# Token stages of a two-layer transformer: the values' tail product on four array tiles, and the second norm's rows on ScalarE

## The chip, the cores and the metric

The kernel runs on one core of a Trainium2 chip. Its time is the device time of one execution, in microseconds (us). The engines have short names here: PE (TensorE, matrix products; PEld is its weight load), DVE (VectorE), ACT (ScalarE), POOL (GpSimd) and SP (SyncE, which issues DMAs). Each runs its own list of instructions strictly in order and waits for the others by semaphores. A matrix product takes a stationary operand (up to 128 rows by 128 columns of the array) and streams a moving one through it, up to 512 columns at a time, into PSUM, which has eight banks of 512 f32 columns on 128 partitions.

## The reference, cut to what matters

Four sequences of 2048 tokens (8192 tokens of width 512) pass through two layers. Each adds a cross attention to a context of 154 keys, then a second part, which is a mixture of experts in the first layer and a light and heavy feed-forward with routing in the second.

```
x = x + attn0(layernorm(x), ctx)          # 16 heads of 32, 154 keys, softmax
x = x + experts(layernorm(x))             # top 8 of 32, gate = layernorm(x) @ gate.T
x = x + attn1(layernorm(x), ctx)
y = layernorm(x)
x = x + light(y) + heavy(y)               # score = y . routing_token
attn:  p = softmax((q k^T * tau + delta) / sqrt(32));  out = (p v) Wo^T + bo
```

Only the two attention stages with the norm behind them are touched here.

## The kernel before, in words

`token_phase` is run twice, once for each layer; `gate` is true in the first. A stage goes through NG = 16 groups of 512 tokens (TG = 4 tiles of 128). A turn i works at the same time on four groups: it prepares the queries of group i + 1 (norm, transposes by `x_turn`, product with wq), does the attention of group i, projects the output of group i - 1 and adds it to x (`residual`), and does the side work of j = i - 2, which is the second norm `z` and, in the first stage, the gate: `z_turn` transposes z on PE, and `gate_parts` multiplies it with the gate's weights.

A turn has 16 units, and each unit is one of the four tiles for one of the four head groups g (four heads each). A unit takes two steps of the counter `at`, which runs from 0 to 31. The order of every engine's work inside a turn is written out by hand in tuples of `at` values (V for the values products, Z for z's transposes, NZ for z's rows, OO and OL for the attention output, PT for the tails' copy, QO for the queries' copy). A smaller number stands earlier in the turn, and within one `at` the order of the `if` lines holds.

For one unit, `scores` (four products of 154 columns into a ring over banks 0 to 2) is followed by `maximum` on DVE, four exponentials with their sums on ACT, `inverse` on DVE and `normalize` on POOL. Then `p_transposes` on PE turns the probabilities of the first 128 keys into bank 4 (four transposes), and DVE or ACT copies them to pTm. The last 26 keys of each head are the tail: POOL packs them for four heads into 104 columns, a fifth transpose turns them into bank 5, and ACT copies them to pTt once per head group. `values` then computes p v for 512 tokens of one head group: one f32 product over the 104 tail rows into all 128 output rows, against a value table `vt` with zeros where the heads don't match, and four f32 products of 32 output rows each over the 128 main keys, which run side by side. Both go to bank 7. ACT copies the result (`o_out`), and DVE subtracts to get its low part (`o_low`). An f32 product is carried out as two passes, so the rows show x2 for the tail product and x8 for the four main ones.

Queries and projections use bank 6 (A_BANK), so each query product waits until ACT has copied the one before it (`query_out`). They are sums of three products of 512 columns (L81 to L83, the helper `product`) for each of four chunks; `streamed` issues two chunks in each odd step.

The second norm: DVE gathers the statistics, POOL computes `rstd` (L607, L609), and DVE writes z = (x - mean) * rstd (L722), four instructions per group, in steps 0, 0, 1, 1 of the first stage and 3, 7, 10, 13 of the second. `z_turn` for the first quarter stands at step 3 on PE and waits for all four rows.

## Time and profile before

| | us |
|---|---|
| median of 3 runs | 3379.52 |
| lowest and highest | 3376.65, 3384.28 |
| the profiled execution, its own time | 3375.24 |
| span of its core in the trace | 3373.5 |

Over the span PE was busy for 94%, DVE for 81%, POOL for 62% and ACT for 46%. The first token stage fills about 105 to 955 us, the experts follow until about 1850 us, the second token stage fills about 1955 to 2740 us, and the rest is the light and heavy part. A turn takes 52.6 us in the first token stage and 50.4 us in the second, and turns repeat almost to the hundredth of a microsecond. Busy time says little about PE here, since its products overlap: the distance between the starts of two products is the measure of what one costs.

### The profile page before, as it was taken

The page shows a single profiled execution, that of the slowest core. Times are in us where ns is not written, and L with a number is a line of the kernel's source. Part 1 is how long each engine was busy: PE and PEld are TensorE (multiplying, and loading weights), DVE is VectorE, ACT ScalarE, POOL GpSimd, SP SyncE. Part 2 cuts the span into 40 slices and gives each one's busy share as a digit, 9 for nine tenths or more (in the row PEclk, how much of TensorE's full clock was granted, in tenths as well). Part 3 has the DMA queues.
Part 4 walks back from the last instruction along what each step waited for, and adds up shares of the span by engine and source line. Part 5 has one row for each costly group of instructions (what it writes and reads, how often), then busy time and mean ns, then how long its engine had stood idle before and what let it go on. Part 6 is the DMA issues. An engine that isn't in the chain of part 4 may idle for free. (4 is left out here: it accounts for less than half of the span.)

```text
span 3373.5 us, 55546 instructions
## 1 busy us (share of the span) xinstructions
PE 3187.6 (94%) x17270; PEld 2498.1 (74%) x17270; DVE 2720.3 (81%) x5412; ACT 1560.8 (46%) x5463; POOL 2097.0 (62%) x2416
## 2 busy tenths in 40 slices
PE   7999999999979999999999699999999969999998
PEld 5677777777647888888888567777777758778886
DVE  4788888889746888888887389999999879967775
ACT  1766666676621111111111377777777745321111
POOL 1766766667635777777777477777777753433333
PEclk8999999999989999999999899999999989999999
DMA  7345454454465666766676444555554457730111
GB/s 219 100 137 169 119 172 134 141 155 134 136 210 131 167 176 165 179 168 166 166 179 155 111 128 135 159 164 144 150 171 136 138 166 287 274 102 13 26 13 25
DMA packets 285026, 491.01 MB, mean 146 GB/s; under 512 B 54258, under 2 KB 75058, under 8 KB 284018
## 3 DMA queue, kind: packets, MB, share of 16 engines
q1 hardware_dynamic: 252146, 409.92, 39.3%
q0 software_dynamic: 32256, 77.65, 12.3%
q8 instruction: 116, 1.90, 0.2%
q14 instruction: 124, 1.02, 0.1%
q10 hardware_dynamic: 384, 0.52, 0.1%
HBM read 250.32 MB, written 136.96 MB: 115 GB/s over the span
## 5 line engine op out<-in xcount | busy, mean ns | idle before, releaser
L984 ACT ACTIVATE c_pr<-ps,t_negmax 128x154 f32<-128x154 f32 x1024 | 384.8, 392 | 197.3 <-DVE t_negmax L731 196.3
L731 DVE TENSOR_REDUCE t_negmax<-ps 128x4 f32<-128x616 f32 x512 | 404.1, 789 | 53.2 <-PE ps L1053 52.7
L984 ACT ACTIVATE t_pr<-ps,t_negmax 128x154 f32<-128x154 f32 x1024 | 384.8, 392 | 107.9 <-DVE t_negmax L731 103.0
L754 DVE COPY t_pTm<-ps 128x512 f32<-128x512 f32 x448 | 306.2, 683 | 118.6 <-PE ps L1066 114.5
L649 POOL TENSOR_TENSOR t_pr<-t_pr,t_inv 128x512 f32<-128x512 f32 x256 | 274.8, 1073 | 191.0 <-DVE t_inv L746 189.9
L649 POOL TENSOR_TENSOR c_pr<-c_pr,t_inv 128x512 f32<-128x512 f32 x256 | 271.7, 1061 | 195.2 <-DVE t_inv L746 193.9
L1053 PE MATMUL ps<-t_kst,t_stack 98*128 98x154 f32 x2048 | 352.8, 291 | 26.7 <-DMA t_stack<-t_q_low 10.0
L1053 PEld LDWEIGHTS ps<-t_kst,t_stack 98*128 98x128 f32 x2048 | 279.5, 193 | 39.1 <-issue 18.3
L81 PE MATMUL ps<-e_xT_high,e_wgu_high 128*128 128x512 f32 x768 | 301.6, 393 | 1.4 <-DVE e_xT_low L1639 1.4
L83 PE MATMUL ps<-e_xT_high,e_wgu_low 128*128 128x512 f32 x768 | 299.3, 390 | 0.0
L82 PE MATMUL ps<-e_xT_low,e_wgu_high 128*128 128x512 f32 x768 | 299.0, 389 | 0.0
L1686 ACT ACTIVATE e_sig<-ps 128x512 f32<-128x512 f32 x96 | 57.3, 597 | 499.4 <-PE ps L83 494.6
L81 PE MATMUL ps<-t_xnT_high,t_wq_high 128*128 128x512 f32 x512 | 221.8, 433 | 18.2 <-ACT t_qT L907 18.2
L2341 POOL TENSOR_TENSOR h_w_low<-c_hw,h_w_high 128x512 fp32r<-128x512 f32 x64 | 89.8, 1403 | 232.8 <-DVE h_w_high L70 232.8
L81 PE MATMUL ps<-t_wo_high,t_oT_high 128*128 128x512 f32 x512 | 218.2, 426 | 0.4 <-DVE c_wide_rows L763 0.4
L984 ACT ACTIVATION_READ_ACCUMULATOR t_pr<-ps,t_negmax 128x1 f32 x1024 | 213.2, 208 | 0.0
L984 ACT ACTIVATION_READ_ACCUMULATOR c_pr<-ps,t_negmax 128x1 f32 x1024 | 212.5, 208 | 0.0
L1296 POOL TENSOR_TENSOR e_wd_low<-c_wd_in,e_wd_high 128x512 fp32r<-128x512 f32 x96 | 131.1, 1391 | 127.2 <-DVE e_wd_high L70 127.2
L621 POOL TENSOR_TENSOR t_q_low<-t_qT,t_q_high 128x512 fp32r<-128x512 f32 x128 | 170.5, 1332 | 54.7 <-DVE t_q_high L70 54.7
L83 PE MATMUL ps<-t_xnT_high,t_wq_low 128*128 128x512 f32 x512 | 203.5, 397 | 0.0
L82 PE MATMUL ps<-t_xnT_low,t_wq_high 128*128 128x512 f32 x512 | 202.6, 396 | 0.0
L83 PE MATMUL ps<-t_wo_high,t_oT_low 128*128 128x512 f32 x512 | 201.4, 393 | 0.0
(359 smaller groups left out, 9313.8 us busy)
## 6 DMA issues: line engine op xcount, KB each, us to landing
t_stack<-t_q_high SPq DMA_DIRECT2D x1016, 64.0 KB, 2.0
c_wgu_in<-in_gate_upT SPq DMA_DIRECT2D x32, 1536.0 KB, 6.4
t_stack<-t_q_low SPq DMA_DIRECT2D x512, 64.0 KB, 2.0
x_dram<-c_wide_rows SPq DMA_DIRECT2D x32, 1024.0 KB, 7.6
c_wd_in<-in_downT SPq DMA_DIRECT2D x32, 768.0 KB, 11.5
t_xbo<-in_x SPq DMA_DIRECT2D x16, 1024.0 KB, 5.7
xw_dram<-t_z SPq DMA_DIRECT2D x16, 1024.0 KB, 5.3
t_xbo<-x_dram SPq DMA_DIRECT2D x16, 1024.0 KB, 11.2
```

The costliest lines, as they stand in the source:

```text
L81: pe.matmul(out, left[0], right[0], start=start, stop=False)
L82: pe.matmul(out, left[0], right[1], start=False, stop=False)
L83: return pe.matmul(out, left[1], right[0], start=False, stop=stop)
L621: pool.tensor_tensor(qlow[:, n % 2, :], qT[:, n % 2, :], qhigh[:, n % 2, :].bitcast(F32), ALU.subtract).then_inc(s["q_low"], 1)
L649: pool.tensor_tensor(main, main, inv[:, v, :].unsqueeze(2).to_broadcast([P, HG, P]), ALU.mult).then_inc(s["normed"], 1)
L731: dve.tensor_reduce(negmax[:, u, :], flat[:, at:at + HG * APART].rearrange("p (h n) -> p h n", h=HG)[:, :, 0:KEYS], AX, ALU.max, negate=Tr ...
L754: dve.tensor_copy(pTm[:, g % 2, :, t * P:(t + 1) * P], ps[:, 4, :].rearrange("p (h n) -> p h n", h=HG)).then_inc(s["pTm"], 1)
L984: op = act.activation(pr[:, u % 4, h, :], flat[:, col:col + KEYS], ACT.Exp, bias=negmax[:, u, h:h + 1], accum_out=total[:, u, h:h + 1])
L1053: mm = pe.matmul(flat[:, at:at + KEYS], stack[:, HG * (g % 2) + h, t * P:(t + 1) * P], kst[:, g, h * KEYS:(h + 1) * KEYS], start=True, sto ...
L1296: pool.tensor_tensor(wd[1][:, f, :], c["wd_in"][:, f, :], wd[0][:, f, :].bitcast(F32), ALU.subtract).then_inc(s["wd_low"], 1)
L1686: act.activation(sig[:, (FC * q + f) % 2, :], ps[:, b, :], ACT.Silu).then_inc(s["silu"], 1)
L2341: pool.tensor_tensor(w1[1][:, m % RING], c["hw1"][:, :, f * P:(f + 1) * P], w1[0][:, m % RING].bitcast(F32), ALU.subtract).then_inc(s["w1" ...
```

## The change

It has two parts.

The first is on the values. The tails of a pair of heads now form a block of 52 rows (PROWS), and the blocks of the two pairs stand at partitions 0 and 64, so a tile's tails take 116 columns. Their transposes leave `p_transposes` and become `tail_transposes`, four in a row once per head group, at the new steps TT. The tail product becomes four products of 64 rows by 64 columns of the array over 256 tokens each: two pairs of heads times two halves of the 512 tokens. So that the four fall on four different tiles, `place` swaps the pairs for the last two token tiles. The output goes to banks 5 and 6, 256 columns each, the main products are split in two halves as well (eight instead of four), and A_BANK moves to bank 7. Bank 5 thus holds the tails' transposes and then half of the output, so the transposes of a group wait for `o_low` of the one before.

The second is on the norm. The rows of z are now made by ACT (`side_rows`, an Identity with scale rstd and bias shift = -mean * rstd), at steps 0, 1, 2, 3 of the first stage and 1, 4, 8, 10 of the second. POOL computes shift with two more small instructions. `z_turn` moves from steps 3, 5, 8 to 4, 6, 9. `residual` and `rstd_of` get a wait for the rows of z. The inverse of the sums is written in place.

```diff
+        def place(h, t):
+
+            return h if t < TG // 2 else (h + 2) % HG
...
-        V = (15, 24, 2, 7) if gate else (15, 23, 3, 6)
+        V = (15, 24, 2, 7) if gate else (15, 23, 1, 7)
+        TT = (12, 20, 30, 5) if gate else (12, 20, 29, 5)
...
-        Z = (3, 5, 8, 22)
+        Z = (4, 6, 9, 22)
...
-        OL = (23, 30, 4, 9) if gate else (17, 27, 5, 9)
+        OL = (18, 27, 4, 9) if gate else (17, 26, 3, 9)
...
-        NZ = (0, 0, 1, 1) if gate else (3, 7, 10, 13)
+        NZ = (0, 1, 2, 3) if gate else (1, 4, 8, 10)
...
-        OO = (16, 26, 2, 7) if gate else (15, 24, 4, 7)
+        OO = (16, 25, 2, 7) if gate else (15, 24, 2, 7)
...
+                    reached(pool, s["z" if gate else "xl"], TG * n)
...
+                    pool.tensor_scalar(shift[:], mv[:, which, :, 0], -1.0, None, ALU.mult).then_inc(s["s_minus"], 1)
+                    pool.wait_ge(s["s_minus"], n + 1)
+                    pool.wait_ge(s["s_rstd"], n + 1)
+                    pool.tensor_tensor(shift[:], shift[:], rstd[:, which, :], ALU.mult).then_inc(s["s_shift"], 1)
...
+                if v % TG == 0:
+                    reached(pool, s["tail_mm"], GROUPS * i + v // TG - 1)
...
+                    reached(dve, s["z" if gate else "xl"], TG * j)
...
+            def side_rows(j, t):
+                act.wait_ge(s["s_shift"], j + 1)
+                if t == 0 and (gate or j < NG - 1):
+                    reached(act, s["z_stored"], 16 * j)
+                if t == 0 and gate:
+                    reached(act, s["z_mm"], DC * j)
+                act.activation(z_of(j)[:, t, 0:D], xs[:, t, :], ACT.Identity, bias=shift[:, t:t + 1],
+                               scale=rstd[:, 1, t:t + 1]).then_inc(s["z" if gate else "xl"], 1)
...
-                if t == 0:
-                    reached(pe, s["pTt"], GROUPS * i + g)
                 for h in range(HG):
-                    pe.transpose(ps[:, 4, h * P:(h + 1) * P], pr[:, v % 4, h, 0:P], ident[:])
-                pe.transpose(ps[0:TROWS, 5, t * P:(t + 1) * P], tails[:, v % 4, :],
-                             ident[:]).then_inc(s["p_mm"], 1)
+                    mm = pe.transpose(ps[:, 4, h * P:(h + 1) * P], pr[:, v % 4, place(h, t), 0:P], ident[:])
+                mm.then_inc(s["p_mm"], 1)
+
+            def tail_transposes(i, g):
+
+                pe.wait_ge(s["normed"], 2 * (UNITS * i + TG * g + TG))
+                reached(pe, s["oT_out"], GROUPS * i + g)
+                for t in range(TG):
+                    at = (HIGH + PROWS) * ((TG * g + t) % 8)
+                    mm = pe.transpose(ps[0:HIGH + PROWS, 5, t * P:(t + 1) * P], tails[:, at:at + HIGH + PROWS], ident[:])
+                mm.then_inc(s["tail_mm"], 1)
...
-                pe.matmul(ps[:, B_BANK, :], vt[:, g * P:(g + 1) * P], pTt[:], start=True, stop=False,
-                          skip_group_check=True)
-                for h in range(HG):
-                    mm = pe.matmul(ps[h * DK:(h + 1) * DK, B_BANK, :], vm[:, g * P + h * DK:g * P + (h + 1) * DK],
-                                   pTm[:, g % 2, h, :], start=False, stop=True, skip_group_check=True)
+                for half in range(2):
+                    for q in range(2):
+                        r = HIGH * (q if half == 0 else 1 - q)
+                        pe.matmul(ps[HIGH * q:HIGH * (q + 1), 5 + half, 0:HALF],
+                                  vt[r:r + PROWS, g * P + HIGH * q:g * P + HIGH * (q + 1)],
+                                  pTt[r:r + PROWS, half * HALF:(half + 1) * HALF], start=True, stop=False,
+                                  skip_group_check=True)
+                for half in range(2):
+                    for h in range(HG):
+                        mm = pe.matmul(ps[h * DK:(h + 1) * DK, 5 + half, 0:HALF],
+                                       vm[:, g * P + h * DK:g * P + (h + 1) * DK],
+                                       pTm[:, g % 2, h, half * HALF:(half + 1) * HALF], start=False, stop=True,
+                                       skip_group_check=True)
...
```

What stands in a row on PE in steps 2 to 5 of a turn of the first stage, before (the L81 to L83 rows are the streamed query products, `t_z` the transposes of z, `c_pr` those of the probabilities):

```order
L1076 MATMUL ps<-t_pTt,t_vt 128x512
L1079 MATMUL ps<-t_pTm,t_vm 32x512 x4
...
L83 MATMUL ps<-t_xnT_high,t_wq_low 128x512
L1038 MATMUL ps<-ident,t_z 128x128 x4
L1065 MATMUL ps<-ident,c_pr 128x128 x4
L1066 MATMUL ps<-ident,t_tails 104x128
L1053 MATMUL ps<-t_kst,t_stack 128x154 x4
L81 MATMUL ps<-t_xnT_high,t_wq_high 128x512
```

and the same place of the change:

```order
L1113 MATMUL ps<-t_pTt,t_vt 64x256 x4
L1119 MATMUL ps<-t_pTm,t_vm 32x256 x8
...
L84 MATMUL ps<-t_xnT_high,t_wq_low 128x512
L1091 MATMUL ps<-ident,c_pr 128x128 x4
L1081 MATMUL ps<-t_kst,t_stack 128x154 x4
L1066 MATMUL ps<-ident,t_z 128x128 x4
L82 MATMUL ps<-t_xnT_high,t_wq_high 128x512
```

The transposes of z moved behind the transposes of the probabilities and the scores of unit 2, the tails' transpose left the row, and the values are two groups of smaller products.

ACT in steps 0 to 4 of the same turn, before (`t_qT` is the queries' copy, `t_oT_high` that of the attention output, each pair of `c_pr` rows the four exponentials of a unit):

```order
L907 ACTIVATE t_qT<-ps,t_bq 128x512 [waits t0_q_low,t0_q_mm]
L984 ACTIVATE c_pr,t_total<-ps,t_negmax 128x154 [waits t0_p_mm,t0_negmax]
L984 ACTIVATE c_pr,t_total<-ps,t_negmax 128x154 x3
L914 CAST t_oT_high<-ps 128x512 [waits t0_proj,t0_pv]
L907 ACTIVATE t_qT<-ps,t_bq 128x512 [waits t0_q_low,t0_q_mm]
L984 ACTIVATE c_pr,t_total<-ps,t_negmax 128x154 [waits t0_p_mm,t0_negmax]
L984 ACTIVATE c_pr,t_total<-ps,t_negmax 128x154 x3
```

and in the change:

```order
L923 ACTIVATE t_qT<-ps,t_bq 128x512 [waits t0_q_low,t0_q_mm]
L971 ACTIVATE t_z<-c_wide_rows,t_shift,t_rstd 128x512 [waits t0_z_mm,t0_z_stored,t0_s_shift]
L1010 ACTIVATE c_pr,t_total<-ps,t_negmax 128x154 [waits t0_p_mm,t0_negmax]
L1010 ACTIVATE c_pr,t_total<-ps,t_negmax 128x154 x3
L971 ACTIVATE t_z<-c_wide_rows,t_shift,t_rstd 128x512 [waits t0_s_shift]
L930 CAST t_oT_high<-ps 128x512 [waits t0_proj,t0_pv]
L923 ACTIVATE t_qT<-ps,t_bq 128x512 [waits t0_q_low,t0_q_mm]
L971 ACTIVATE t_z<-c_wide_rows,t_shift,t_rstd 128x512 [waits t0_s_shift]
L1010 ACTIVATE c_pr,t_total<-ps,t_negmax 128x154 [waits t0_p_mm,t0_negmax]
L1010 ACTIVATE c_pr,t_total<-ps,t_negmax 128x154 x3
L971 ACTIVATE t_z<-c_wide_rows,t_shift,t_rstd 128x512 [waits t0_s_shift]
```

Four rows of z now stand between the copies and the exponentials, the third and the fourth of them behind the second copy of the queries.

PE at the start of a turn of the second stage, before:

```order
L1065 MATMUL ps<-ident,t_pr 128x128 x4
L1066 MATMUL ps<-ident,t_tails 104x128
L1053 MATMUL ps<-t_kst,t_stack 128x154 x4
...
L83 MATMUL ps<-t_xnT_high,t_wq_low 128x512
L1076 MATMUL ps<-t_pTt,t_vt 128x512
L1079 MATMUL ps<-t_pTm,t_vm 32x512 x4
L1065 MATMUL ps<-ident,t_pr 128x128 x4
```

and in the change:

```order
L84 MATMUL ps<-t_xnT_high,t_wq_low 128x512
L1113 MATMUL ps<-t_pTt,t_vt 64x256 x4
L1119 MATMUL ps<-t_pTm,t_vm 32x256 x8
L1091 MATMUL ps<-ident,t_pr 128x128 x4
L1081 MATMUL ps<-t_kst,t_stack 128x154 x4
```

The values of head group 2 moved from behind unit 1's scores and query products (step 3) to in front of those scores (step 1).

## Rows read from the trace of the kernel before

**Rows 1.** Stretches of the token stages: busy us by engine, clock, DMA share, GB/s

```profile
105.00:955.00 850.00, 818.49 (x5024) 610.99 (x5022) 714.46 (x1636) 563.32 (x2320) 577.26 (x759) 0.99 0.49 143
1955.00:2740.00 785.00, 754.42 (x4535) 566.56 (x4528) 725.56 (x1483) 604.29 (x2404) 582.21 (x686) 1.00 0.50 145
```

**Rows 2.** Waits of PE in 105 to 955 us: us in total, times, longest

```profile
PE ps L1065 <- DVE t_pTm L754: 11.0, 15, 1.8
```

**Rows 3.** The same view in 1955 to 2740 us

```profile
PE ps L81 <- ACT t_qT L907: 12.2, 15, 0.9
```

**Rows 4.** Timeline of PE, one values step: start us, us, engine, line, operation

```profile
412.88 0.40 PE L83 MATMUL ps<-t_wo_high,t_oT_low 128*128 128x512 f32 x1
413.12 1.02 PE L1076 MATMUL ps<-t_pTt,t_vt 104*128 104x512 f32 x2
414.07 1.06 PE L1079 MATMUL ps<-t_pTm,t_vm 128*32 128x512 f32 x8
415.07 0.66 PE L1065 MATMUL ps<-ident,c_pr 128*128 128x128 f32 x4
```

**Rows 5.** Timeline of PE around the first side transposes of a turn, first token stage

```profile
446.74 0.39 PE L83 MATMUL ps<-t_xnT_high,t_wq_low 128*128 128x512 f32 x1
446.97 0.60 PE L1038 MATMUL ps<-ident,t_z 128*128 128x128 f32 x4
447.40 0.60 PE L1065 MATMUL ps<-ident,c_pr 128*128 128x128 f32 x4
447.84 0.27 PE L1066 MATMUL ps<-ident,t_tails 128*104 128x128 f32 x1
447.87 0.75 PE L1053 MATMUL ps<-t_kst,t_stack 98*128 98x154 f32 x4
448.45 0.43 PE L81 MATMUL ps<-t_xnT_high,t_wq_high 128*128 128x512 f32 x1
```

**Rows 6.** Timeline of ACT in the same stretch

```profile
447.17 0.69 ACT L907 ACTIVATE t_qT<-ps,t_bq 128x512 f32<-128x512 f32 x1 [0.97 <-PE ps L83]
447.75 0.38 ACT L984 ACTIVATE c_pr<-ps,t_negmax 128x154 f32<-128x154 f32 x1
...
449.21 0.60 ACT L919 COPY t_pTt<-ps 104x512 f32<-104x512 f32 x1
```

**Rows 7.** Groups by line, 105 to 955 us: busy us, mean ns, idle before

```profile
L722 DVE TENSOR_SCALAR t_z<-c_wide_rows,t_mv,t_rstd 128x512 f32<-128x512 f32 x64 | 45.0, 746 | 0.0
```

**Rows 8.** The same view in 1955 to 2740 us

```profile
L722 DVE TENSOR_SCALAR t_z<-c_wide_rows,t_mv,t_rstd 128x512 f32<-128x512 f32 x60 | 63.1, 1051 | 0.0
...
L961 ACT ACTIVATE t_z<-t_z,t_rn 128x512 f32<-128x512 f32 x56 | 39.6, 735 | 15.6 <-POOL t_rn L686 15.6
```

**Rows 9.** Timeline of POOL at the end of a turn, first token stage

```profile
436.50 0.20 POOL L607 TENSOR_TENSOR t_ve<-t_mv,t_eps 128x4 f32<-128x4 f32 x1 [2.03 <-DVE t_mv L717]
436.78 1.02 POOL L609 TENSOR_TENSOR t_rstd<-t_ve,t_half 128x4 f32<-128x4 f32 x1
437.77 1.04 POOL L649 TENSOR_TENSOR c_pr<-c_pr,t_inv 128x512 f32<-128x512 f32 x1
438.77 0.38 POOL L651 TENSOR_TENSOR t_tails<-c_pr,t_inv 128x104 f32<-128x104 f32 x1
```

**Rows 10.** Timeline of PE there

```profile
439.47 0.60 PE L1065 MATMUL ps<-ident,c_pr 128*128 128x128 f32 x4
```

**Rows 11.** Timeline of PE at the start of a turn, second token stage

```profile
2472.00 0.65 PE L1053 MATMUL ps<-t_kst,t_stack 98*128 98x154 f32 x4
...
2473.92 1.02 PE L1076 MATMUL ps<-t_pTt,t_vt 104*128 104x512 f32 x2
...
2476.88 0.43 PE L81 MATMUL ps<-t_xnT_high,t_wq_high 128*128 128x512 f32 x1
```

**Rows 12.** Timeline of ACT there

```profile
2473.71 0.39 ACT L984 ACTIVATE t_pr<-ps,t_negmax 128x154 f32<-128x154 f32 x1 [1.37 <-DVE t_negmax L731]
...
2475.18 0.70 ACT L907 ACTIVATE t_qT<-ps,t_bq 128x512 f32<-128x512 f32 x1
```

More of the change, by code:

```diff
@@ L414, in last, with halves @@
             return isinstance(j, int) and j == NG - 1
+        def place(h, t):
+            return h if t < TG // 2 else (h + 2) % HG
+        def halves(v):
+            return v.rearrange("p (b n) -> p b n", b=2)
         def o_bank(j, t):
@@ L596, in _ @@
             pool.memset(eps[:], EPS).then_inc(s["ready"], 1)
+            pool.memset(tails[:], 0.0).then_inc(s["ready"], 1)
             if gate:
@@ L601, in _ @@
                 pool.memset(c["z_last"][:, :, D:XS], 0.0).then_inc(s["ready"], 1)
[L602 removed]
+            pool.wait_ge(s["ready"], 3 if gate else 5)
             def rstd_of(which, kind, n):
                 pool.wait_ge(s[kind + "_mv"], TG * n + TG)
+                if kind == "s":
+                    reached(pool, s["z" if gate else "xl"], TG * n)
                 pool.tensor_tensor(ve[:, which, :], mv[:, which, :, 1], eps[:], ALU.add).then_inc(s[kind + "_ve"], 1)
@@ L1012, in turn @@
                         x_turned(i + 1, XT.index(at))
+                    if at in NZ and prev2:
+                        side_rows(j, NZ.index(at))
                     if at in ZA and gate and prev2:
@@ L1189, in turn @@
                         streamed(st)
+                    if at in TT[:3] and cur:
+                        tail_transposes(i, TT.index(at))
+                    if at == TT[3] and prev:
+                        tail_transposes(i - 1, GROUPS - 1)
                     if at in V[:2] and cur:
```

86 lines of the change are left out of this document (42 added, 44 removed).

## The prediction

> **What bounds the kernel now.** I read the busy times of the two token stages first, since nothing else of the kernel is edited except small work at its start. PE is busy for 818 of 850 us in the first stage and 754 of 785 us in the second, at full clock; DVE follows with 714 and 726, and ACT has 563 and 604 [rows 1]. PE's waits are short and repeat once a turn: 11.0 us in 15 waits for DVE's copy of the probabilities in the first stage [rows 2], and 12.2 us in 15 waits for ACT's copy of the queries in the second [rows 3]. So a stage is PE's list of products end to end plus some 2 us of waits in a turn of 50. A product saved on PE is time saved, but only as long as PE doesn't wait for something else afterwards. The question is therefore what each part takes from PE's list, and which wait the new places of ACT's work put into it.
>
> **The values.** Before, one values step takes 415.07 - 413.12 = 1.95 us from the first tail product to whatever follows [rows 4]. Four transposes of 128 columns take 447.84 - 447.40 = 0.44 us [rows 5], so 128 f32 columns cost 0.11 us and a pass of 512 costs 0.44. Two passes for the tails and two for the main keys (four products side by side) make 1.76 us, and the remaining 0.19 goes with the two changes of the array's division, about 0.10 each. Afterwards there are two passes of 256 columns for the tails, if the four tiles run side by side, and four of 256 for the main keys: 6 x 0.22 = 1.32 us. The divisions change three times, 0.29 us. That gives 1.61 us and a saving of 0.34. More pass boundaries, and weight loads that have only 0.22 us to hide under, take something back. No row shows their price; I bound it by 0 and by two more changes (0.20), and take 0.07, nearer to nothing, since the eight products of a values step already start together in rows of 1.06 us [rows 4]. The saving is 0.27 us a step (0.14 to 0.34), 1.08 a turn with four steps, 17 us a stage with 64. The tails' transposes are still four in a head group at 0.11 us each; they move and cost nothing more. Their new wait for the low part of the former output is hidden: ACT's and DVE's steps for it are over two units (some 6 us) before, except at step 5, where I still find 3 us between.
>
> A page bears on how the tiles share banks. The first two tail products come from row halves 0 and 64 of the array and both write bank 5, on partitions 0 to 63 and 64 to 127. The Trainium skill, TensorEngine Tiling (Array Packing), Restrictions and Gotchas, says that different row tiles cannot access the same PSUM bank simultaneously. No row here has row tiles, so the trace can't say; by that rule the tails cost what the first rival says.
>
> **The second norm's rows, first stage.** DVE loses 64 instructions of 746 ns, 45 us in all [rows 7]. DVE doesn't bound there, and its chain in front of the one regular wait [rows 2] (norm of x, copies, the second query cast) starts from PE's own transposes and isn't shortened. ACT gains as many, and I price them by its scaling of such rows from and to SBUF in the other stage: 735 ns, the next starting about 0.62 us after it [rows 8]. What matters is where they stand. Before, the query product of step 3 ends and the transposes of z follow at once, at 446.97 [rows 5], all z rows being done. ACT copies the queries at 447.17, begins the four exponentials of unit 1 at 447.75 and has them behind it at 449.21, 1.46 us later [rows 6]. Afterwards the third z row stands between the copy and the exponentials, the fourth behind them, and PE's transposes of z wait for the fourth. With the values 0.27 us shorter: copy at 446.90, third row at 447.48, exponentials at 448.10, fourth row at 449.56, done at 450.30. PE comes from the query product at 446.70, has 0.44 us of transposes and some 0.49 of scores, and would begin z's transposes at 447.62. It waits until 450.30, 2.7 us (on the way, the last of the scores waits for the first exponential, which is part of this). Before, this place lost 0.1 us [rows 5] (the scores took 0.58). So +2.6 us a turn. Nothing wins it back: the chain runs from PE through ACT to PE, and what DVE does later in the turn starts from PE's next transposes.
>
> POOL's two new instructions take about 0.28 us each, as its small one does (436.50 to 436.78), and stand in front of a unit's normalization that ends at 439.15 [rows 9], for which PE comes at 439.47 [rows 10]. About 0.5 later, less 0.3 of slack: +0.2 us a turn (0 to 0.5).
>
> A turn of the first stage: 2.6 + 0.2 - 1.08 = +1.7 us. 14 turns carry z rows beside attention: +24. Two turns have attention but no z rows: -2. First stage: **+22 us** (with a saving of 0.34 and no POOL term, +15; with 0.14 and 0.5, +33).
>
> **The second stage.** Here nobody waits for z early, and the rows stand apart. DVE, 92% busy, loses 63 us [rows 8], which shortens few of PE's waits, since those listed are for ACT [rows 3]. But the values of head group 2 move in front of unit 1's scores. Those started at 2472.00 [rows 11] and start 1.68 - 0.11 = 1.57 later. The exponentials of unit 1 go from 2473.71 [rows 12] to 2475.28, and the queries' copy behind them, 2475.18 before, to 2476.74, done at 2477.35. PE's next query product, at 2476.88 before [rows 11], is ready by 2476.39 (less 0.27, and two tail transposes of 0.11 that moved), so it waits 0.9 us. The values of group 3 move behind the query product of step 7, and their output copy stands before the queries' copy on ACT: 0.6 + 0.7 us after the values end, against 0.44 + 0.49 us of PE's work, a wait of 0.4. Together 1.3 - 1.08 = +0.2 us a turn: **+3 us** over 15 turns. If the relief of DVE takes 1 us a turn off the waits that remain, it is -13; if z rows and squares hold exponentials up once more in a turn, +12.
>
> **Start and ends.** In the last turns the four rows lie on ACT among its squares, where DVE made them beside it: 4 x 0.62 = 2.5 us, of which some is hidden: +2 us. POOL's clearing of the tails and two fewer DMAs for the value table lie beside the loading of inputs: 0 (-1 to +1).
>
> **The sum.** 22 + 3 + 2 = +27 us on the profiled execution's 3375.24: 3402. The median of the runs is 4.3 us above that execution, and the highest 9; I add half of the 4.3: **3404 us**.
>
> **Rivals.** (1) The four tiles don't run side by side, because pairs in one bank take turns: two more passes of 0.22 in each of 128 steps, +56 us, 3460. Against it: the four column tiles of the main product do share one bank now [rows 4]. Chance 0.08; it carries the page's rule. (2) Nearly even: the wait for z is there, but DVE's relief, 108 us over both stages [rows 7, 8], takes some 1 us a turn off the other waits, and the values save the full 0.34. 3404 - 16 - 9, about 3379. For it: DVE is the releaser in [rows 2]. Against: the DVE work in front of those waits isn't what is taken away. Chance 0.18. (3) Faster: ACT's rows bind nowhere, and only the saving is left, 128 x 0.27 = 35 us, 3340. It decides at the fourth row of z: if that is done before PE has finished the scores of unit 2, that is within 0.93 us of the query product's end, there is no wait; by the rows of ACT it takes 3.6. PE would have to carry 2.7 us less wait later in the turn, and the waits it has are about that long. Chance 0.12. (4) The second stage waits more for ACT, at 77% busy before and some 5 points more after: 3425. Chance 0.04. The forecast keeps 0.58.
>
> **How the numbers follow.** Leaving out (1) at the top and (3) at the bottom leaves 0.8: 3368, the low end of (2), to 3430, above (4) and the forecast's own upper bounds (22 to 33 and 3 to 12 make +20 on 3404). About 0.2%, 6.8 us, is what a measurement can tell from no change: 3372.8 to 3386.3. Faster takes (3) and 0.06 of (2); within takes the rest of (2) and 0.03 of the forecast: 0.15; slower takes the remainder, 0.67.
>
> **What would show it.** In the trace after, PE's transposes of z should wait about 1.7 us in each turn of the first stage for ACT's z rows, and the scores before them about 1 us for the exponentials; a first-stage turn should take 54.3 us instead of 52.6. The values step should take 1.68 us, with four tail products starting within hundredths of each other; if they start in two pairs 0.4 us apart, rival 1 holds. In the second stage the query product behind unit 2 should wait 0.9 us for its copy and the turn stay near 50.4 us. The forecast is wrong if the transposes of z don't wait, or if a turn of the first stage gets shorter.

## The result

The changed kernel takes 3429.99 us (median of 4, 3422.78 to 3435.32), the kernel before in the same comparison 3381.90 (median of 4, 3376.65 to 3390.04). The ratio is 1.0139, with a 95% interval of 1.011 to 1.0167: slower by some 48 us. The direction was forecast, but only +24.5 us of it (3404 against the median of 3379.52 that stood before); 3429.99 lies at the upper end of the range, 3368 to 3430. The profiled execution after is the fastest of its kernel (span 3421.0 us against 3373.5, +47.5).

The split by stage comes from the first and the last score matmul of each: the first token stage 838.6 to 870.9 us (+32.3), the second 798.7 to 811.7 (+13.0), between and around them +2.2. The forecast had +22, +3 and +2. All turn times below are measured from the first score matmul of unit 0 to that of the next turn. By that measure a turn of the first stage took 53.3 us before, not the 52.6 that the prediction gives; its "54.3 instead of 52.6" should be read as "+1.7". Nor do the turns of before all repeat to the hundredth: inner turns take 53.3 to 54.3 us in the first stage and 50.4 to 51.6 in the second.

The stretches of the changed kernel that answer to [rows 1], then two of its turns and one of before's (length, then busy us of PE, PEld, DVE, ACT, POOL, granted clock, DMA share, GB/s):

```profile
105.00:985.00 880.00, 809.55 (x5902) 626.59 (x5901) 676.09 (x1570) 606.67 (x2385) 572.26 (x789) 0.98 0.47 138
1985.00:2790.00 805.00, 744.99 (x5439) 575.72 (x5437) 692.91 (x1443) 647.50 (x2477) 575.27 (x721) 1.00 0.49 142
```

```profile
617.80:672.50 54.70, 51.18 (x384) 39.81 (x382) 44.13 (x104) 39.19 (x155) 36.96 (x52) 1.00 0.46 137
782.70:839.80 57.10, 53.04 (x383) 41.22 (x382) 44.35 (x104) 39.21 (x155) 36.98 (x52) 0.97 0.45 135
```

```profile
707.60:760.90 53.30, 52.23 (x327) 39.35 (x325) 46.37 (x108) 36.47 (x151) 37.14 (x50) 1.00 0.57 161
```

The work moved as the change says: DVE has 2 us less in a turn and ACT 3 more, and PE has 1 us less. The turn got longer all the same. PE's waits in the first stage (to be read against [rows 2]) and in the second (against [rows 3]):

```profile
PE ps L1066 <- ACT t_z L971: 26.3, 16, 4.4
PE ps L1081 <- ACT c_pr L1010: 19.4, 31, 1.1
PE ps L1091 <- DVE t_pTm L778: 10.2, 15, 0.7
```

```profile
PE ps L82 <- ACT t_qT L923: 34.5, 44, 1.0
PE ps L1081 <- ACT t_pr L1010: 15.1, 32, 1.2
```

The first two lines are the forecast wait for z's rows. Both are new: before, the first stage has no regular wait of the z transposes and 0.3 us in one wait for the exponentials. In the second stage the wait for the queries' copy has gone from 12.2 us in 15 waits to 34.5 in 44. A values step on PE, where [rows 4] shows one of before:

```profile
675.49 0.66 PE L1113 MATMUL ps<-t_pTt,t_vt 52*64 52x256 f32 x8
676.08 1.07 PE L1119 MATMUL ps<-t_pTm,t_vm 128*32 128x256 f32 x16
677.08 0.50 PE L82 MATMUL ps<-t_xnT_high,t_wq_high 128*128 128x512 f32 x1
```

It takes 677.08 - 675.49 = 1.59 us instead of 1.95. The four tail products take 0.59 us together, and their first passes begin within 0.02 us (675.489 to 675.509); had those of one bank taken turns, four passes of 0.22 would have made 0.88. So rival 1 is out: two row halves wrote one bank here, on different partitions, side by side. By the rule that it carried (the Trainium skill, TensorEngine Tiling (Array Packing), Restrictions and Gotchas) they would have taken turns; for this product the measurement decides against it.

The place in the first stage on which the forecast rests, PE and then ACT, in a turn of 54.7 us:

```profile
678.94 0.54 PE L1081 MATMUL ps<-t_kst,t_stack 98*128 98x154 f32 x3
680.59 0.34 PE L1081 MATMUL ps<-t_kst,t_stack 98*128 98x154 f32 x1 [1.11 <-ACT c_pr L1010]
682.40 0.55 PE L1066 MATMUL ps<-ident,t_z 128*128 128x128 f32 x3 [1.47 <-ACT t_z L971]
```

```profile
678.78 0.69 ACT L923 ACTIVATE t_qT<-ps,t_bq 128x512 f32<-128x512 f32 x1 [0.98 <-PE ps L84]
679.37 0.80 ACT L971 ACTIVATE t_z<-c_wide_rows,t_shift,t_rstd 128x512 f32<-128x512 f32 x1
680.07 0.38 ACT L1010 ACTIVATE c_pr<-ps,t_negmax 128x154 f32<-128x154 f32 x1
...
681.53 0.82 ACT L971 ACTIVATE t_z<-c_wide_rows,t_shift,t_rstd 128x512 f32<-128x512 f32 x1
```

```profile
L971 ACT ACTIVATE t_z<-c_wide_rows,t_shift,t_rstd 128x512 f32<-128x512 f32 x64 | 52.1, 822 | 2.1 <-POOL t_shift L630 2.1
```

The last line is the group of all such rows in the first stage, 105 to 985 us (busy us, mean ns). This is the chain as forecast: queries' copy, third row, exponentials, fourth row, z's transposes.

A turn of 57.1 us has the same two waits, of the same length. What differs is what follows them:

```profile
793.05 0.48 PE L82 MATMUL ps<-t_xnT_high,t_wq_high 128*128 128x512 f32 x1
793.36 0.41 PE L83 MATMUL ps<-t_xnT_low,t_wq_high 128*128 128x512 f32 x1
793.60 0.60 PE L84 MATMUL ps<-t_xnT_high,t_wq_low 128*128 128x512 f32 x1
794.00 0.63 PE L82 MATMUL ps<-t_xnT_high,t_wq_high 128*128 128x512 f32 x1
794.42 0.63 PE L83 MATMUL ps<-t_xnT_low,t_wq_high 128*128 128x512 f32 x1
794.85 0.63 PE L84 MATMUL ps<-t_xnT_high,t_wq_low 128*128 128x512 f32 x1
```

Passes of 512 columns start 0.23 us apart at first and then 0.43: the granted clock has fallen to its lower level, 1.2 GHz, and the turn's mean is 0.97. Four of the 13 turns between 174 and 895 us are so, and PE is busy 1.2 to 1.7 us longer in them. The last turn of the stage stands at 0.94. In the kernel before, no turn of the stage behind the first is below 1.00.

Against the same turns of the kernel before, the nine with full clock are longer by 1.6 us on average (0.5 to 2.3), the four with the fall by 2.7 to 3.75 and the last one by 4.6; the first two together by 0.5. So of the +32.3 us some 22 are what the turns cost at full clock, as forecast, and some 10 go with the fallen clock.

### The profile page after: what moved, and what is told of

Same layout as the page of the kernel before. It is cut to its first block and busy times, and to the rows that moved or that the text cites. A ratio compares the mean times of both kernels' runs of the same rounds, so it can differ in the third digit from the quotient of the medians.

```text
span 3421.0 us, 59457 instructions
## 1 busy us (share of the span) xinstructions
PE 3163.5 (92%) x19062; PEld 2520.8 (74%) x19062; DVE 2642.1 (77%) x5284; ACT 1645.4 (48%) x5591; POOL 2083.4 (61%) x2482
## 3 DMA queue, kind: packets, MB, share of 16 engines
q0 software_dynamic: 32256, 77.65, 12.2%
## 5 line engine op out<-in xcount | busy, mean ns | idle before, releaser
L668 POOL TENSOR_TENSOR t_pr<-t_pr,t_total 128x512 f32<-128x512 f32 x256 | 274.9, 1074 | 212.8 <-DVE t_total L770 211.4
L668 POOL TENSOR_TENSOR c_pr<-c_pr,t_total 128x512 f32<-128x512 f32 x256 | 271.0, 1058 | 215.3 <-DVE t_total L770 215.1
L83 PE MATMUL ps<-e_xT_low,e_wgu_high 128*128 128x512 f32 x768 | 299.3, 390 | 0.0
L83 PE MATMUL ps<-t_xnT_low,t_wq_high 128*128 128x512 f32 x512 | 204.4, 399 | 0.0
L83 PE MATMUL ps<-t_wo_low,t_oT_high 128*128 128x512 f32 x512 | 201.1, 393 | 0.0
```

The source lines that it names most:

```text
L83: pe.matmul(out, left[0], right[1], start=False, stop=False)
L668: pool.tensor_tensor(main, main, total[:, v, :].unsqueeze(2).to_broadcast([P, HG, P]), ALU.mult).then_inc(s["normed"], 1)
```

## The experiments

The theory after this comparison: in the first stage the rows on ACT cost a wait of 3 us a turn and now and then a fall of the clock; in the second stage the new place of the values costs. The rival: one part alone carries the loss in both. The table gives, for each kernel, the median time and from its trace the two stages and their usual turn (us). Each ratio is against the kernel before in the same comparison; its medians there lay from 3378.7 to 3381.9. The turn is one that recurs in the stage, with full clock (58.0 is the exception: that kernel has none with full clock; the 53.8 is one with fallen clock). It is mostly the shortest kind. The average over the fourth to the fifteenth of the first stage's 16 turns is 53.5 us before, 55.6 changed, 53.35 for the values only, 53.6 for z later and 53.0 for the values with xbo first (xbo is what the residual adds: the load of x's rows comes earlier there).

| kernel | time | ratio, 95% | first stage, turn | second stage, turn |
|---|---|---|---|---|
| before | 3381.9 | 1 | 838.6, 53.3 | 798.7, 50.4 |
| changed | 3430.0 | 1.011 to 1.0167 | 870.9, 54.7 | 811.7, 51.5 |
| values only | 3401.2 | 1.0046 to 1.0074 | 838.8, 52.6 | 823.2, 52.3 |
| rows only | 3451.5 | 1.0198 to 1.0225 | 908.0, 58.0 | 794.3, 50.1 |
| fill in the waits | 3425.4 | 1.0113 to 1.0144 | 867.6, 54.7 to 56.0 | 813.4, 51.6 |
| z later | 3397.4 | 1.0033 to 1.006 | 842.3, 52.6 | 813.9, 51.6 |
| group 2 back | 3433.3 | 1.0151 to 1.0186 | 878.0, 55.2 | 810.5, 50.4 to 53.8 |
| rows only, with fill | 3429.5 | 1.0132 to 1.0161 | 882.4, 56.5 | 795.5, 50.1 |
| values only, xbo first | 3395.2 | 1.0031 to 1.0057 | 832.6, 52.9 | 824.0, 52.3 |
| place only | 3404.5 | 1.0062 to 1.0086 | 840.5, 53.3 | 821.2, 52.0 |
| put together | 3371.0 | 0.9961 to 0.9982 | 836.3, 53.1 | 793.4, 49.9 |
| rows in second stage only | 3375.9 | 0.9983 to 1.0001 | 839.0, 53.3 | 794.7, 50.1 |
| put together, scaling later | 3367.8 | 0.995 to 0.9977 | 832.6, 52.9 | 786.6, 49.4 |
| before, no tail product | 3348.9 | 0.989 to 0.992 | 822.9, 51.7 | 790.0, 49.7 |

### The two halves apart

The changed kernel with the rows given back to DVE and `Z`, `ZD`, `ZA`, `NZ` and `SQ` as before (`ZD` and `ZA` are the steps at which DVE and ACT copy z's transposes out of PSUM, `SQ` those of ACT's squares):

```
-                    if at in NZ and prev2:
-                        side_rows(j, NZ.index(at))
...
+                        for t in range(TG):
+                            if at == NZ[t]:
+                                normed(1, "s", j, xs, z_of(j), "z" if gate else "xl", (t,))
```

> The changed kernel with the second half of the change taken back: the normalized rows are made by VectorE again, in the places of before; the split tail product and the tails' transposes once per group stay. Theory (the rows on ScalarE are what costs, the values part is a gain): the first stage has no wait of about 1.5 us before z's transposes and its turns are near 53.3 - 4 x 0.35 = 51.9 us; the second stage gains at most 1.4 us a turn, less if VectorE (busy 372.2 of 398 us before) becomes late; 3340 to 3365 us in all, faster than both kernels. Rival (the values part brings nothing because other engines are as late as PE): turns of 53.3 and 50.4 us as before, 3375 to 3385 us. Second rival (the values part costs as well, by its larger evictions and POOL's strided tails): above 3390 us.

And the kernel before with the rows alone:

> The kernel before with only the second half of the change: the normalized rows on ScalarE in the places of the changed kernel, POOL's two steps for the negated mean, z's transposes and evictions at the changed kernel's steps; tails and values as before. Theory (the two halves add up: the rows cost about 3 us of waits a turn in the first stage, now and then a fall of the granted clock behind them, and 1 to 2.5 us a turn in the second): first-stage turns of 56 us, 3445 to 3475 us in all. Rival (most of the rows' cost exists only because the values part has put other evictions of ScalarE into the same steps): first-stage turns near 54.5, 3395 to 3425 us.

Measured: 3401.2 and 3451.5. The first is a miss; the time lies in the second rival's range, but the place of the values, tested below, and not larger evictions or POOL's strides, gives most of it. The second falls in its range, though not by the parts expected: 58.0 us a turn in the first stage instead of 56, and a gain in the second instead of a loss. The values part, meant to save PE's time, is slower by itself, and wholly in the second stage: 823.2 us against 798.7, 52.3 us a turn against 50.4, with the same waits for the queries' copy as the changed kernel:

```profile
PE ps L82 <- ACT t_qT L924: 31.8, 41, 1.0
PE ps L1080 <- ACT t_pr L1011: 12.6, 26, 0.8
```

The rows cost nothing there: alone they make the second stage shorter by 4.4 us. In the first stage it is the other way about: the values part makes the usual turn 0.7 us shorter where it saves PE 1.4 (the average turn only 0.2, in part for a reason found below), and the rows alone cost 4.7 us a turn. They do so by waits of 2.0 and 1.0 us in all 13 inner turns (160 to 900 us), and in every one of these turns the granted clock falls:

```profile
PE ps L1047 <- ACT t_z L953: 25.5, 13, 2.0
PE ps L1062 <- ACT c_pr L991: 13.1, 13, 1.0
```

```profile
699.30:757.40 58.10, 54.33 (x328) 40.55 (x326) 44.26 (x104) 39.27 (x156) 37.23 (x52) 0.97 0.45 135
```

So the loss of the first stage is the rows', that of the second the values'. The halves don't add: 19.5 and 69.8 us alone, 48.1 together. With the values part the z wait is shorter (1.5 us against 2.0) and most turns keep their clock.

### Does standing still cost the clock?

The same edit in the changed kernel (8 and 12 transposes) and in the kernel with the rows alone (6 and 14). Bank 3 is where z's transposes go next:

```
+            def filler(j, n):
+                pe.wait_ge(s["logit"], j + 1)
+                pe.wait_ge(s["xnT_low"], DC * (j + 3))
+                for m in range(n):
+                    pe.transpose(ps[:, T_BANK, (m % TG) * P:(m % TG + 1) * P], ident[:], ident[:])
...
                 if k == 0:
+                    filler(j, 12)
                     pe.wait_ge(s["z"], TG * (j + 1))
```

> The changed kernel with work for TensorE put into the two waits of the first stage's turns: 8 transposes of the identity ahead of the last score matmul of unit 2 and 12 ahead of z's transposes, into the bank that z's transposes then overwrite. Both groups are shorter (0.9 and 1.3 us) than the waits there (1.3 and 1.7 us beyond the usual distance), so they should cost nothing by themselves. Theory (the fall of the granted clock to one half in four of the turns, 227.9, 338.6, 506.6 and 782.7, comes from TensorE's standing still just before): no turn with a granted clock under 0.99, four turns shorter by 1.7 us and the last one too, 7 to 10 us less than the changed kernel, so 3420 to 3424. Rival (the clock falls by something that has nothing to do with the waits): the same turns at 0.97 and 3428 to 3432 us. If the filler delays the real work, above 3435.

> The kernel before with the rows on ScalarE, as in the run of the rows alone (3451), and with 6 and 14 transposes of the identity in the two waits of 1.2 and 2.2 us in each turn of the first stage. There the granted clock is 0.97 or less in each of the turns that has these waits, and its passes of 512 columns take 427 ns for some 3 us behind them. Theory (standing still makes the clock fall, and this fall is a third of what the rows cost in the first stage): granted clock 1.00 in these turns, 56.3 instead of 58.0 us a turn, 13 turns, 3425 to 3432. Rival (the slow passes have another cause, such as the load of DMA or ScalarE at this place): clock 0.97 as before, 3448 to 3455.

Measured in the kernel with the rows alone: 3429.5 us, 22 less than without the fill, and the turn goes from 58.0 to 56.5 us, at full clock in every turn after the first:

```profile
682.30:738.90 56.60, 55.05 (x348) 41.28 (x345) 44.27 (x104) 39.27 (x156) 37.25 (x52) 1.00 0.44 127
```

In the changed kernel no turn after the first is below 1.00 either, and the last one takes 48.5 us instead of 52.6. The time is 4.6 us less, short of the 7 to 10 expected; its first turn took 51.7 us against 48.3, and without it the stage is 6.7 us shorter. That the fall follows PE's standing still is shown by the kernel with the rows alone (22 us). (The Trainium skill, TensorE: Matmul & The Clock Gate, The HAM clock gate, describes these two levels and that an idle array gets the lower one; the traces agree on the levels, with 0.43 and 0.23 us a pass, and here waits of 1 to 2 us are all the idleness that stands before a fall.) What decides between two turns with equal waits isn't: it fell in 4 inner turns of the changed kernel's trace and in 7 of the kernel with group 2 moved back, whose first stage has the same code. It fell behind a single wait too: one of 1.5 us for DVE's copy (at 400.6 us in the kernel without the tail product), one of 1.65 (at 2327.6 in the version put together) and one of 2.3 (at 2175.4 in the kernel with group 2 moved back). The other three executions of the changed kernel had a mean clock of 0.974 to 0.975 against 0.979 in the profiled one and took 7 to 13 us longer. So its median probably holds more falls than its trace.

### The wait for the fourth row

```
-        Z = (4, 6, 9, 22)
+        Z = (6, 8, 10, 22)
-        ZD = (5, 11)
+        ZD = (7, 11)
-        ZA = (7, 24)
+        ZA = (9, 24)
```

> The changed kernel with z's first three transposes of the first stage two steps, two steps and one step later (6, 8 and 10 in place of 4, 6 and 9) and their evictions with them (VectorE 7, ScalarE 9), so that the fourth row, which ScalarE finishes 0.2 us before they start now, has two steps more. Theory (the wait for the fourth row is half of what the rows cost, and is only a matter of its place): the 1.5 us before z's transposes go and nothing is late in their stead, the wait of 1.1 us for the exponentials stays, the granted clock falls less; first-stage turns near 53.2, 3398 to 3410 us. Rival (ScalarE is behind by its own work in steps 1 to 5, and PE only meets it somewhere else): PE waits for p copies, query copies or exponentials instead, 3420 to 3430 us.

Measured: 3397.4 us, 33 less, just under the range. PE's waits from 160 to 850 us:

```profile
PE ps L1081 <- ACT c_pr L1010: 14.5, 13, 1.1
PE ps L1066 <- ACT t_zT L954: 6.3, 13, 0.5
PE ps L1091 <- POOL t_tails L674: 5.9, 4, 1.9
```

The wait for z's rows is gone, and that for the exponentials stays. A smaller one stands in its stead, for ACT's copy of z's first transposes (0.5 us a turn). The wait for DVE's copy of the probabilities, 12.3 us in 12 with the values part alone over the same time, is gone too. The usual inner turn takes 52.6 us, as with the values part alone. So the loss was a matter of place: with the rows on ACT and z two steps later, the first stage (842.3) is within 3.5 us of the one with the rows on DVE (838.8).

### What costs in the second stage

Two runs take the place of the values step and its product apart. The place alone, in the kernel before:

```
-        V = (15, 24, 2, 7) if gate else (15, 23, 3, 6)
+        V = (15, 24, 2, 7) if gate else (15, 23, 1, 7)
-        OO = (16, 26, 2, 7) if gate else (15, 24, 4, 7)
+        OO = (16, 26, 2, 7) if gate else (15, 24, 2, 7)
-        OL = (23, 30, 4, 9) if gate else (17, 27, 5, 9)
+        OL = (23, 30, 4, 9) if gate else (17, 26, 3, 9)
```

> The kernel before with its own values product and rows, and only the places of the second stage moved as the change has them: values of group 2 at step 1 instead of 3 and of group 3 at 7 instead of 6, output copies at 2 and 7, low parts at 3 and 9. It is the other half of the run that puts group 2 back. Theory (the place costs by itself): TensorE waits 1.2 us behind unit 2's scores and 0.4 before the projection, a turn of the second stage takes 51.6 to 52.2 us instead of 50.4, 3398 to 3408. Rival (the place is harmless and the split product costs): 50.4 us a turn and 3380 to 3384.

And the split product with group 2 at its old place:

```
-        V = (15, 24, 2, 7) if gate else (15, 23, 1, 7)
+        V = (15, 24, 2, 7) if gate else (15, 23, 3, 8)
-        TT = (12, 20, 30, 5) if gate else (12, 20, 29, 5)
+        TT = (12, 20, 30, 5) if gate else (12, 20, 29, 6)
-        OO = (16, 25, 2, 7) if gate else (15, 24, 2, 7)
+        OO = (16, 25, 2, 7) if gate else (15, 24, 4, 8)
```

> The changed kernel with the values of head group 2 of the second stage back at step 3, where before had them (ScalarE's output copy at 4, VectorE's at 5), and group 3 behind them: its tails at step 6, its values at 8, copies at 8 and 10. Nothing else is moved. In the changed kernel TensorE stands still 1.2 us in each turn behind unit 2's scores, since the values no longer lie between the third query product and the fourth. Theory (in the second stage the place of this step costs, not the split product): that wait goes, a turn takes about 50.3 us instead of 51.5, 15 turns bring 15 to 20 us, 3408 to 3415. Rival (the turn is set by VectorE and ScalarE with the split product wherever it stands): 51.3 to 51.6 us a turn, 3425 to 3432.

The place alone costs 1.6 us a turn, 22.4 us in the stage, as expected, with the waits of the changed kernel (27.8 us in 43 for the queries' copy). It is the larger part of the answer. The waits make 1.1 of the 1.6 us in an inner turn; PE's own list is 0.5 us longer as well (49.5 against 49.0 us busy), which no run follows up. Before, the values of group 2 lay between the third query product and the fourth and covered the copy of the third. At step 1 they cover nothing, and the copy begins 8.5 us into the turn instead of 6.6 besides. In the changed kernel:

```profile
2468.59 0.66 PE L1081 MATMUL ps<-t_kst,t_stack 98*128 98x154 f32 x4
2470.25 0.50 PE L82 MATMUL ps<-t_xnT_high,t_wq_high 128*128 128x512 f32 x1 [1.01 <-ACT t_qT L923]
...
2477.50 0.50 PE L82 MATMUL ps<-t_wo_high,t_oT_high 128*128 128x512 f32 x1 [0.29 <-ACT t_qT L923]
...
2505.22 0.34 PE L1081 MATMUL ps<-t_kst,t_stack 98*128 98x154 f32 x1 [0.76 <-ACT t_pr L1010]
```

These are the two forecast waits (0.9 and 0.4 us) and one that wasn't. In all, the waits of this turn come to 3.5 us, those of a turn before to 1.3 (0.82 for the queries' copy and 0.46 for the exponentials). Of the 2.2 more, 1.3 were forecast. The other 0.9 are longer or new waits for the exponentials, the first copy of the queries and DVE's copy. Those for the exponentials come with the split product, not with the rows: 12.6 us in 26 waits with the values part alone, 6.1 in 13 with the place alone. So this is where the time that it saves on PE goes.

Putting group 2 back took the wait of 1.01 us away (14.6 us in 15 remain, which before has too) and gave nothing, a miss: 51.4 us a turn on average over the inner turns with full clock, and 1.2 us in the whole stage. (The time of the whole kernel is longer by what its first stage lost to the clock.) In its place stands a wait for which the profile names no releaser, ahead of the scores of unit 4:

```profile
PE ps L1081 <- issue: 16.9, 16, 2.4
PE ps L82 <- ACT t_qT L923: 14.6, 15, 1.0
```

```profile
2588.22 0.65 PE L1081 MATMUL ps<-t_kst,t_stack 98*128 98x154 f32 x4 [2.44 <-issue]
```

Unit 4 is the first of its group and needs the stack of group 1, the queries' parts as DMAs lay them out for the scores. The queue issues the last transfers of the low part until 2584.5 us, and these land a median of 3.6 us later, at 2588.1:

```profile
L485 SPq DMA_DIRECT2D t_stack<-t_q_low x4: 588/590/591, 2582.6 to 2584.5; - x4
...
DMA to landing us min/median/max: 3.4/3.6/4.5
```

So this is, by the times, the stack's transfer; the same sum fits a short wait in another turn (2482.1 + 2.0 to 2.6, the scores at 2484.18). Unit 4's scores start 14.6 us into the turn before, when the values of group 3 stand ahead of them; with those behind, PE is there after 12.5 us and waits until 12.9 to 15.2.

### How much of PE's saving arrives

> The kernel before without the tail keys' product in both stages (the tails are still normalized, transposed and copied, but not multiplied with the values; the attention over them is left out of the result). It takes from TensorE a pass of 0.44 us and one change of the array's division (0.10) in each of 128 values steps, 2.2 us a turn, and from no other engine anything. Theory (TensorE is the busiest engine but the turn is held by the loop through maximum, exponentials, normalization and copy, so what is saved on TensorE comes back as waits): the second stage's turn goes from 50.4 to no less than 49.8, the first's from 53.3 to about 52.3, 3353 to 3365. Rival (TensorE's list is the turn): 48.2 and 51.1 us a turn, 3312 to 3325.

Measured: 3348.9 us, a little under the theory's range and far above the rival's. Some 0.54 x 128 = 69 us were taken from PE and 31 arrive by the medians, 25 by the two traces. The usual turn is 1.6 us shorter in the first stage and 0.7 in the second, of 2.2. The stages as a whole gain 15.7 and 8.8 us of some 35 each, which is less, 1.0 and 0.5 a turn: the first turns of a new batch gain 0.5 to 0.8 us in the first stage, and in two inner turns of the first stage and one of the second the granted clock fell to 0.97. The rest stands in waits (1968 to 2680 us; before, the same lines have 1.7 and 6.1 us), and in others for DVE that come up (8.5 us in 22):

```profile
PE ps L1053 <- issue: 11.0, 13, 3.0
PE ps L1053 <- ACT t_pr L984: 8.4, 13, 0.6
```

### A load that POOL waits for

```
+                if cur:
+                    load_xbo(i)
                 if nxt and cur and (i + 1) % PER == 0:
                     load_values(sp, i + 1, 0)
...
-                if cur:
-                    load_xbo(i)
```

> The kernel with the values part alone (3401) and one order of the first stage's DMA queue changed: the load of the residual's rows goes ahead of the loads of the next batch's values and keys. With the values part POOL waits for this load in the first turn of each new batch (10.0 us in 3 times, 4.4 before), and TensorE's p transposes wait for POOL; those turns take 54.2 to 55.3 us instead of 52.6. Theory (the value table's third load in each group, and the earlier pace, put this load behind): the three turns take 52.6 to 53 us, 4 to 6 us less, near 3396. Rival (the queue waits for something ahead of these loads anyway): no difference, 3399 to 3403, or slower where the keys or values now come late.

Measured: 3395.2 us, 6 less; the two intervals overlap, but in the traces the first stage, the only one touched, is 6.2 us shorter. POOL's wait for the load falls from 10.0 us in 3 times to 0.2 in one, and the turns of 54.2 to 55.3 us are gone. That this load came late is shown. Why it did with the values part (two DMAs for the value table in a group where there was one, or the shorter turn) isn't taken apart.

### A version from these runs

> A version put together from what the runs show. First stage: the split product, the rows on VectorE as before, the residual's load ahead of the next batch's values (as in the run with that order, whose first stage took 832.7 us against 838.6 before). Second stage: the split product, the rows on ScalarE, and the values of group 2 at step 3 again, those of group 3 at step 7 (with their tails at 6), their output copy at 8, behind the queries' copy. With group 3 at step 8 the scores of unit 4 started so early that they waited for the stack's transfers (16.9 us in 16 waits); at 7 its product lies in front of them again. Theory (both covers are back: the product of group 2 hides one query copy, that of group 3 hides the stack's transfer): no wait behind unit 2's scores, no waits of 1 to 2.7 us ahead of unit 4's, turns of 49.6 to 50.4 us, 3352 to 3370 in all. Rival (the stack's transfer sets the turn as long as TensorE is quick in steps 1 to 7): waits ahead of unit 4's scores stay at 0.5 us or more a turn, 50.5 to 51.5 us a turn, 3372 to 3390.

> The kernel before with one thing of the change: in the second stage alone the normalized rows are made by ScalarE. The first stage is the one of before, values and tails too. In the run of the rows alone the second stage took 794.3 us instead of 798.8 and the first lost 69. Theory (the rows are harmless where nothing waits for z early): first stage 838.6 as before, second 794 to 795, 3374 to 3378 in all, at the edge of what can be measured. Rival (the second stage was quicker there only because the first handed it another start): 798 to 799 us and 3378 to 3382.

> The version put together (3371) with one more step moved in its second stage: ScalarE scales the four z rows at steps 25 to 28 instead of 24 to 27. At step 24 ScalarE stands still 1.1 us for POOL's reciprocal norm, then scales a row for 0.7 us, and only then begins the exponentials whose maximum has long been there; TensorE waits 0.75 us for them in each turn, and some tenths twice more. Theory (this chain takes most of what the split product saves in the second stage): the exponentials go first, POOL's norm is there when ScalarE asks for it, turns of 49.2 us instead of 49.9, 3360 to 3366. Rival (the time is only met elsewhere, since the chain from the maxima over the exponentials to the transposes sets the pace): 49.8 to 50.0 us a turn, 3368 to 3373.

Measured: 3371.0 us (1 above the theory's range), 3375.9 (as expected) and 3367.8 (between the theory and the rival, at the upper one's edge). With both covers back the split product is quicker than the whole one in the second stage, but by 0.2 us a turn (49.9 against 50.1 with the rows on ACT and the places of before), not by the 1.4 that PE saves. What holds it was read from the version's trace: ACT waits for POOL's reciprocal norm, scales a row and only then begins the exponentials.

```profile
2456.01 0.72 ACT L994 ACTIVATE t_z<-t_z,t_rn 128x512 f32<-128x512 f32 x1 [1.09 <-POOL t_rn L710]
2456.64 0.37 ACT L1018 ACTIVATE t_pr<-ps,t_negmax 128x154 f32<-128x154 f32 x1
```

One step later for the scaling brings PE's waits for the exponentials from 12.8 us to 5.4 and a turn to 49.4. Of the 0.7 us expected 0.5 arrived, and the two intervals overlap, so of the time as a whole this step alone isn't shown. Both versions beat both kernels, the last by 0.23 to 0.5%. The rows on ACT in the second stage alone can't be told from no change in the time, but the stage is 4.0 us shorter, as expected.

## Why the prediction was right in its direction and wrong in its size

Two steps failed. The sum credited the values' full saving, 1.08 us a turn, to the second stage, where none or next to none of it arrived; and it put the granted clock behind the new waits at nothing, which was some 10 us. They make up the difference between +27 and the +47.5 of the two traces.

- **The wait for z's rows, first stage.** Right. 2.7 us were forecast; the extra distance in the timeline is 1.28 us ahead of the last score matmul and 1.70 ahead of z's transposes, 2.98 together. The row on ACT was taken at 0.62 us to its successor, from an operation with one operand per partition [rows 8]; this one has two and takes 0.80 to 0.84, the next starting 0.70 later. (The Trainium skill, ScalarE: Activation LUTs, What ACT_TABLE_LOAD costs, gives some 0.09 us for each such operand; the trace agrees, with 822 ns against 735.)
- **The values.** The saving was forecast at 0.27 us a step with 0.34 as its bound and is 0.36, 1.44 a turn: the seams between passes cost nothing. "A product saved on PE is time saved, but only as long as PE doesn't wait for something else afterwards" was written, and then the sum took the full 1.08 us a turn in both stages. In the first stage it happened to hold, probably since there the chain through the fourth row starts from PE and moves earlier with it: the two kernels with the waits filled, without and with the split product, differ by 1.4 us a turn on average (836.8 and 816.0 us for the 15 turns behind the first). With the rows on DVE the same product is worth 0.2 us on average, 0.5 with the residual's load ahead. In the second stage it is worth -0.3 to 0.2.
- **POOL's two instructions.** Forecast at +0.2 us a turn. They take 0.24 and 0.20 us, and PE's wait for the tails is 4.0 us in 4 times where it was 3.8 in 4: nothing.
- **A first-stage turn at full clock.** Forecast +1.7 us; +1.4 in the usual turn, +1.6 on average. Partly luck: the wait is 0.4 longer than summed, the saving 0.36 larger, and POOL's 0.2 isn't there.
- **The clock.** No term, and no case for it among the rivals. In the trace it makes four turns longer, by 6 to 7 us together, and the last one by some 3; more in the median. That is the step from +22 to +32.
- **The second stage.** The two waits were forecast at 0.9 and 0.4 us and are 1.0 and 0.3; the new places as a whole cost 1.6 a turn in the run of the places alone. The turn was forecast at +0.2 and is +1.1. By the runs: place +1.6, product -0.2 to +0.3, rows -0.3 to -0.8. The product was put at -1.08: this is the term that failed, and with it +3 became +13.
- **Start and ends.** +2 forecast, +2.2 measured.
- **Rivals.** (2) needed DVE's relief to take waits off PE. The rows alone show such relief in the second stage, 0.3 us a turn instead of 1. Its sum was off as well: 1 us a turn in both stages would be 30 us and not 16. (3) fell with the fourth row. (4), 3425 for a second stage that waits more for ACT, came nearest in size, with a chance of 0.04. But the cause wasn't ACT's load: the rows on ACT shorten that stage.

Left open: the first turn of the first stage took 45.6 to 51.7 us in different kernels at a granted clock of 0.81 to 0.89, 48.3 in the changed one and 46.8 before. No run was made for it.

## What to carry to other kernels

Work taken from the busiest engine is worth its full time only if that engine waits for nothing behind it. Where it is 95% busy and each turn holds loops through other engines and transfers, leave some of its work out once and see how much arrives; here it was 1.6 and 0.7 of 2.2 us in the usual turn and less over the stage. What arrives also depends on which wait bounds: in the first stage the same split product was worth 1.4 us a turn ahead of the chain through z's rows and 0.2 without that chain. A product that stands between another product and the use of its copy is cover: moving it brings out the wait that it hid (1.0 us here), whichever engine's load seems to be the reason. A wait of PE's that is new has its own length and, behind it, possibly slow passes: price both.

## What was not expected of the hardware

- Waits of 1.1 and 1.5 us, a score matmul apart, were followed by a fall of the granted clock to 1.2 GHz for some 3 us in 4 of 13 turns, and in 7 of 13 of another kernel's trace with the same code there. With 1.0 and 2.0 us it was 13 of 13. With transposes in the gaps it was none.
- Two row halves of TensorE wrote one PSUM bank on different partitions side by side: four products of 256 f32 columns in 0.59 us.
- In the second stage of the kernel with group 2 moved back, the stack's transfers of 64 KB land 2.0 us after their issue in the median, but 3.6 us (3.4 to 4.5) in a turn behind the loads of a new batch, with the DMA engines 76% busy (2580 to 2589 us). An order that is just in time at 2.0 is late there.
